# Two-layer transformer on one core: splits after all maxima, first GpSimd addition before the pairs, rows normalised later, a new end of the first layer, and ScalarE copying a fifth block

## What is computed

```python
x = x + ln(attn0(ln(x)))      # 32 query heads of 16, one key/value head, ALiBi bias, causal softmax
x = x + ln(ffn0(ln(x)))       # one 512x512 matrix (block-quantised codes times scales) and a bias
x = x + ln(attn1(ln(x)))      # 32 heads of 128, 8 low-rank key/value heads, partial rotary embedding
x = x + ln(ffn1(ln(x)))       # octonion-structured ternary gate, up and down matrices, silu
```

## Time and profile before

| | |
|---|---|
| median of 3 runs | 2241.18 us (2239.95 to 2243.91) |
| the profiled execution's own time | 2244.26 us |
| span of its profile | 2242.3 us |
| PE busy | 2064.2 us (92%) |
| DVE busy | 1767.8 us (79%) |
| ACT busy | 1389.1 us (62%) |
| POOL busy | 936.3 us (42%) |
| mean granted PE clock | 0.973 of full |

### The profile page before, as it was taken

One profiled execution on the slowest core, in us unless ns is written; L12 is line 12 of the kernel. 1 busy time (PEld: TensorE's weight loads), 2 busy tenths in 40 slices (PEclk: granted clock), 3 DMA queues, 4 the chain that ended last, 5 costly groups with the idle time before them and its releaser, 6 DMA issues. The chain is left out here.

```text
span 2242.3 us, 48569 instructions
## 1 busy us (share of the span) xinstructions
PE 2064.2 (92%) x18563; PEld 1248.5 (56%) x18563; DVE 1767.8 (79%) x3711; ACT 1389.1 (62%) x3037; POOL 936.3 (42%) x901
## 2 busy tenths in 40 slices
PE   7678989898757799999999999999999999988998
PEld 3356666566524466665666666556565665534443
DVE  5689999999665787787787778878778877977665
ACT  2455665656545687787687777777777776762222
POOL 0067786879833233333323323333323323253221
PEclk9799999999878999999999999999999999999999
DMA  5201010101113444434453454354354344520100
GB/s 203 79 16 36 13 51 17 54 10 47 27 65 89 84 68 91 90 68 93 89 94 66 90 100 82 68 91 91 68 94 90 66 85 78 102 76 19 38 20 38
DMA packets 390214, 153.81 MB, mean 69 GB/s; under 512 B 358544, under 2 KB 369424, under 8 KB 387936
## 3 DMA queue, kind: packets, MB, share of 16 engines
q1 hardware_dynamic: 389984, 150.71, 30.9%
HBM read 48.69 MB, written 11.53 MB: 27 GB/s over the span
## 5 line engine op out<-in xcount | busy, mean ns | idle before, releaser
L1777 POOL TENSOR_TENSOR q_in_sbuf<-q_in_sbuf,sinq 128x512 f32<-128x512 f32 x128 | 162.6, 1271 | 722.0 <-ACT q_in_sbuf L1909 598.4
L1921 ACT ACTIVATE xp<-xp,nm 128x128 f32<-128x128 f32 (+3 forms) x512 | 281.4, 551 | 199.1 <-DVE nm L2004 199.1
L1803 PE MATMUL bank<-xT_hi,weights_and_hi 128*128 128x512 f16 x1280 | 382.5, 381 | 7.5 <-DVE yacc L2019 4.8
L823 ACT ACTIVATE weights_and_hi<-bank,unit 128x512 f32<-128x512 f32 x320 | 214.3, 688 | 175.0 <-PE bank L622 172.5
L1886 ACT ACTIVATE probs_hi<-xp,rl 128x128 f16<-128x128 f32 (+3 forms) x512 | 245.2, 550 | 67.9 <-DVE rl L2024 64.3
L1973 DVE SCALAR_TENSOR_TENSOR probs_lo<-xp,rl,probs_hi 128x128 f16<-128x128 f32 (+3 forms) x512 | 282.6, 614 | 0.0
L1981 DVE TENSOR_TENSOR q1T_lo<-qf,q1T_hi 128x512 f16<-128x512 f32 x128 | 88.5, 691 | 225.0 <-ACT q1T_hi L1900 225.0
L2004 DVE CUSTOM_DVE_ANT_0 xp<-bank,mask,cs 128x128 f32<-128x128 f32 (+3 forms) x512 | 250.5, 546 | 0.0
L1803 PE MATMUL bank<-xT_lo,weights_and_hi 128*128 128x512 f16 x640 | 243.6, 381 | 0.0
L540 POOL CAST weights_and_hi<-weights_and_hi 128x1024 f16<-128x1024 f32 (+1 forms) x192 | 188.5, 996 | 121.2 <-ACT weights_and_hi L823 120.6
L1803 PE MATMUL bank<-p1T_hi,v_hi 128*128 128x128 f16 x1280 | 221.9, 219 | 3.3 <-DMA p1T_lo<-probs_lo 3.3
(11 more groups left out here) (307 smaller groups left out, 5499.3 us busy)
## 6 DMA issues: line engine op xcount, KB each, us to landing
weights_and_hi<-in_wq SPq DMA_DIRECT2D x8, 1024.0 KB, 5.9
raw_o<-in_wo SPq DMA_DIRECT2D x8, 1024.0 KB, 5.9
x_front<-in_x SPq DMA_DIRECT2D x4, 1024.0 KB, 6.5
q_stack<-q_hi SPq DMA_DIRECT2D x64, 64.0 KB, 2.6
xb<-in_x SPq DMA_DIRECT2D x4, 1024.0 KB, 5.3
wup<-in_wup SPq DMA_DIRECT2D x3, 1024.0 KB, 12.1
fused_scratch<-weights_and_hi SPq DMA_DIRECT2D x12, 256.0 KB, 3.0
x_scratch<-xb SPq DMA_DIRECT2D x3, 1024.0 KB, 4.3
```

The lines of the kernel that those rows point to most:

```text
L823: act.activation(px[:, p % 2, i, :], bank_of(("x", p, i))[:, :], ACT.Exp, scale=unit[:, 0:1]).then_inc(s_ed, 1)
L1777: pool.tensor_tensor(qs[:, i % 2, :], qs[:, i % 2, :], rope["sink" if u[0] == "k" else "sinq"][:, :], ALU.mult).then_inc(s_rot, 1)
L1803: ins = pe.matmul(out, lhs(a), rhs(c), start=(first and i == 0), stop=(last and i == 2))
L1921: ins = act.activation(x, x, ACT.Exp, scale=-1.0, bias=nm[:, m % 3, t:t + 1], accum_out=ls[:, m % 3, t:t + 1])
```

## The change

1. **Setup.** The four clamps and reciprocals come first, then the constants, then the low halves in a row. PE transposes batch 0's rows before it waits for the next part of `wup`, not after. SP no longer waits for the stored tiles at the end of the setup. The wait is moved to the first exponential and to the later loads, which needs the slopes' scratch in a tensor of its own.
2. **POOL.** One small addition (`first_sum`) at the start of the layer, whose result nothing reads.
3. **Fifth block.** ACT copies its high half one step later, behind the first exponential of the next pair. POOL keeps the subtraction, one step later, ahead of its casts.
4. **Rows.** ACT normalises rows 0, 1 at the start and 2, 3 at the end of step +2 (before: 0, 1 at the end of +1, and 2, 3 at the start of +2).
5. **End.** The steps stop at n = 73. The last transposes of heads (`o`, 3) come a step earlier, batch 2's last `f` tile a step later, and in the steps after the last scores the reciprocals of the sums come before the evacuations. Batch 2's `a2` and `n3` and the last batch's `y` are woven into the tail by hand on all engines. The last batch has its own residual rows `xl` (the memory of the front rows, loaded early), its own `yl` (that of the normed heads) and own statistics. The tail uses all eight banks. The next layer's splits move to its end.

```diff
@@ split_matrices, DVE
                 dve.reciprocal(rg[:, i:i + 1], gm[:, i:i + 1]).then_inc(s_rg, 1)
-                dve.wait_ge(s_rg, i + 1)
+            after.get("vector", nothing)(dve)
+            dve.wait_ge(s_rg, len(jobs))
+            for i, job in enumerate(jobs):
                 dve.wait_ge(s_hi, i + 1)
@@ FusedUpProjections
         for i, (m, n) in enumerate(self.tiles):
-            pe.wait_ge(self.s_ld[n + 1], 16)
             if i == 4:
                 rows.transpose(pe, self.bank[4:8])
+            pe.wait_ge(self.s_ld[n + 1], 16)
...
-        sp.wait_ge(self.s_o, 16 * len(self.tiles))
@@ layer0, POOL
+                pool.tensor_tensor(first_sum[:, :], C["mhalf"][:, 0:TT], C["mhalf"][:, 0:TT], ALU.add)
...
-                    for i, (c0, c1) in enumerate(((0, 2), (2, 4), (4, 5))):
+                    for i, (c0, c1) in enumerate(((0, 2), (2, 4))):
                         pool.wait_ge(*emptied[("x", p, c1 - 1)])
                         pool.tensor_copy(ph[0][:, p % 2, c0:c1, :], px[:, p % 2, c0:c1, :]).then_inc(s_wh, 1)
-                    pool.wait_ge(s_wh, 3 * p + 3)
+
+                def last_weights_lo(p):
+                    pool.wait_ge(s_w4, p + 1)
                     pool.tensor_tensor(ph[1][:, p % 2, 4, :], px[:, p % 2, 4, :], ph[0][:, p % 2, 4, :],
                                        ALU.subtract).then_inc(s_wc, 1)
@@ layer0, ACT
+                    if (p, i) == (0, 0):
+                        act.wait_ge(K0.s_stored, K0.STORED)
...
+                def last_weights_hi(p):
+                    if p >= 2:
+                        act.wait_ge(s_pf, p - 1)
+                    act.wait_ge(*emptied[("x", p, 4)])
+                    act.activation(ph[0][:, p % 2, 4, :], px[:, p % 2, 4, :], ACT.Copy).then_inc(s_w4, 1)
...
+                        if i == 0 and 0 <= n - X_LAG - 1 < NP:
+                            last_weights_hi(n - X_LAG - 1)
...
-                        for u in norms_at(n - 2) if i < 2 else norms_at(n - 1) if i > 2 else ():
-                            normalise(u, i + 2 if i < 2 else i - 3)
+                        for u in norms_at(n - 2) if i != 2 else ():
+                            normalise(u, i if i < 2 else i - 1)
@@ layer0, order of the end
-        STEPS = range(-6, NP + 17)
+        STEPS = range(-6, NP + 10)
...
+            late = {("f", LAST - 1, TT - 1): 41, ("o", LAST, TT - 1): 24}
...
-        END = ([("g1", LAST, 0), ("g2", LAST, 0)] + [(k, LAST, t) for k, t in (("n2", 0), ("n2", 1), ("f", 0), ("n2", 2), ("f", 1), ("n2", 3), ("f", 2),
-                                          ("f", 3))] + [("n3", LAST, t) for t in range(TT)])
+        L = LAST
+        END = [("y", L, 0), ("y", L, 1), ("g1", L, 0), ("y", L, 2), ("y", L, 3), ("g2", L, 0), ("n2", L, 0), ("n2", L, 1),
+               ("f", L, 0), ("f", L, 1), ("n2", L, 2), ("n2", L, 3), ("n3", L - 1, 0), ("f", L, 2), ("n3", L - 1, 1),
+               ("n3", L, 0), ("n3", L - 1, 2), ("f", L, 3), ("n3", L, 1), ("n3", L - 1, 3), ("n3", L, 2), ("n3", L, 3)]
...
-        groups = {"s": banks[0:3], "x": banks[3:5], "rest": banks[5:8], "end": banks[0:5]}
+        groups = {"s": banks[0:3], "x": banks[3:5], "rest": banks[5:8], "end": banks}
...
+        sc.sems.append(K0.s_stored)
```

More of the change, by code:

```diff
@@ L352, in others @@
             for kind in ("y", "f"):
-                for t, w in enumerate(BACK[kind]):
-                    b = at(n, w)
-                    if b is not None and has(kind, b):
-                        out.append((kind, b, t))
+                out += [(kind, b, t) for t in range(TT) for b in range(B)
+                        if n == PAIRS * b + offset(kind, b, t) and has(kind, b)]
             if at(n, FRONT["V"]) is not None:
@@ L363, in others @@
                         out += [(kind, b, 2 * i), (kind, b, 2 * i + 1)]
-            for t, w in enumerate(BACK["o"]):
-                if at(n, w) is not None:
-                    out.append(("o", at(n, w), t))
+            out += [("o", b, t) for t in range(TT) for b in range(B) if n == PAIRS * b + offset("o", b, t)]
             return out
@@ L490, in _ @@
                     b = at(n, NORM["a2"] + 4)
[L491 to L493 removed]
+                    if b is not None and has("a2", b):
+                        store_rows(b)
                     if n == NP + V_LAG:
@@ L712, in fill @@
                     else:
-                        rows = {"n1": xf, "n2": ya, "n3": yb}[kind]
-                        if u in END:
+                        rows = yl if (kind, b) == ("n3", LAST) else {"n1": xf, "n2": ya, "n3": yb}[kind]
+                        if b == LAST and kind != "n1":
                             ready = (s_tn, tail_no[1 if kind == "n2" else 3, u[2]])
@@ new lines, in _ @@
+                ahead = LAST - 1
+                evacuate(("y", LAST, 0))
+                for t in range(3):
+                    normalise(("a2", ahead), t)
+                evacuate(("y", LAST, 1))
+                tail_rows(0, 0)
+                evacuate(("y", LAST, 2))
+                tail_rows(0, 1)
+                evacuate(("y", LAST, 3))
+                normalise(("a2", ahead), 3)
+                tail_rows(1, 0)
+                tail_rows(0, 2)
+                hi4(("n2", LAST, 0))
@@ new lines, in _ @@
+                hi4(("n3", ahead, 1))
+                hi4(("n3", LAST, 0))
+                N1.high(act, 0)
+                tail_rows(3, 1)
+                hi4(("n3", ahead, 2))
+                normalise(("n3", ahead), 3)
+                tail_rows(2, 2)
+                hi4(("n3", LAST, 1))
+                tail_rows(2, 3)
+                hi4(("n3", ahead, 3))
+                tail_rows(3, 2)
+                N1.high(act, 1)
+                hi4(("n3", LAST, 2))
+                tail_rows(3, 3)
@@ L884, in _ @@
+                hi4(("n3", LAST, 3))
             @block.vector
@@ L1080, in _ @@
[L1080 to L1100 removed]
+                    tail_statistics(k + 1, t, xl)
@@ new lines, in _ @@
+                N1.reciprocals(dve, bank_of(("g2", LAST, 0)))
+                tail_y(3)
+                ahead_statistics(3)
+                lo4(("n2", LAST, 0))
+                variance(("n3", ahead))
+                tail_add(0, 2)
+                lo4(("n2", LAST, 1))
+                tail_add(0, 3)
+                tail_f(0)
+                tail_f(1)
+                lo4(("n2", LAST, 2))
+                tail_add(2, 0)
+                lo4(("n2", LAST, 3))
+                lo4(("n3", ahead, 0))
@@ L1102, in layer0 @@
+                tail_add(2, 1)
+                tail_f(2)
+                lo4(("n3", ahead, 1))
+                lo4(("n3", LAST, 0))
+                tail_f(3)
+                lo4(("n3", ahead, 2))
+                lo4(("n3", LAST, 1))
+                tail_add(2, 2)
+                lo4(("n3", ahead, 3))
+                tail_add(2, 3)
+                N1.low(dve, 0)
+                lo4(("n3", LAST, 2))
+                N1.low(dve, 1)
+                lo4(("n3", LAST, 3))
         clear(nc, sc.sems)
@@ L2557, in build @@
                                {"sync": other_loads, "tensor": lambda pe: fuse.multiply(pe, rows),
-                                "scalar": lambda act: fuse.copy(act, range(4, len(fuse.tiles)))},
-                               {"vector": rows_and_constants})
+                                "scalar": lambda act: fuse.copy(act, range(4, len(fuse.tiles))),
+                                "vector": rows.constants},
+                               {"vector": rows_low})
                 clear(nc, ss.sems)
```

199 lines of the change are left out of this document (124 added, 75 removed).

## The result

The changed kernel takes 2226.1 us (median of 4 runs, 2223.77 to 2229.5), the kernel before beside it 2240.56 (2237.97 to 2243.91). The ratio is 0.9937, 95% interval 0.9921 to 0.9953. So the change gains 14.5 us, where 30.7 were forecast: the side was right, the size less than half, outside the range of 2197 to 2224. The profiled execution took 2229.5 us (span 2227.7). One of the seven executions of before_sum, a kernel further down, took 4235.99 us; without it its median would be 2235.1 us, not the 2235.63 given there.

The account below looks back on a forecast made before the run. The prediction took DVE to set the pace in the steady pairs (95% busy), PE close behind (90%), and the end to be a chain of waits. Its terms summed to -30.7 us, from 2241.2 to 2210 us, range 2197 to 2224.

Parts of the forecast that it names:

- Term 1: Setup: reordered work lets the layer begin at 57.6 us instead of 66.4, with PE last; -8.8 us.
- Term 2: Start of the layer: POOL's added instruction takes its 7.13 us stall early, so DVE's 5.88 us wait goes; -5.9 us.
- The rival in which it does nothing: Start of the layer: the stall comes back at the old place, the addition gains 0; 2216 us, chance 0.02.
- Term 3: Steady pairs, 125 to 560 us: old DVE waits on POOL go, new meetings of their subtractions cost more; +2 us.
- the stated ends of -12 and +14: Steady pairs: -12 if copies lose nothing, +14 if meetings cost more and PE falls behind.
- The old lock waits: Steady pairs: 17.9 us in 29 DVE instructions that begin during POOL's fifth-block subtraction, expected to go.
- The meetings that the prediction priced at 20 us: Steady pairs: POOL's subtraction against DVE's second subtraction, 6 us, and around DVE's copies of maxima, 14 us.
- The copy on ACT: Steady pairs: 64 new copies of 0.6 us each lie in ACT's idle time; 0, or +4 in the bad case.
- Term 4: Pairs after the last scores: seven fifth-block casts of 7.3 us leave POOL's chain, part of the wait stays; -4.5 us.
- Term 5: End of the layer: weaving the last two batches fills DVE's waits; -14 us, with +0.5 for a second barrier.
- PE behind ACT: Rival, steady pairs: ACT's new copy holds up exponentials and so PE's banks, +19 on the forecast; 2229 us, chance 0.02.
- Slower than before: Rival, pairs: POOL's subtraction comes first against one of DVE's in every pair, 74 us; +23, 2264 us, chance 0.03.

Follow-up runs that it names:

- before_sum: The kernel before with only POOL's small addition (`first_sum`) behind the memsets: 2235.63 us, ratio 0.9967.
- before_setup: The kernel before with only the setup's part of the change: 2233.26 us, ratio 0.9962.
- lo_ahead: The changed kernel with POOL's fifth-block subtraction moved ahead of the two casts of its step: 2204.4 us, ratio 0.9838.
- the part alone: The kernel before with only the fifth block's part: copy on ACT, POOL's subtraction behind the next pair's casts: 2260.88 us, ratio 1.008.
- lo_first: The changed kernel with POOL's fifth-block subtraction first in its step, also ahead of row additions, roots and head scaling: 2200.46 us, ratio 0.9819.
- copy_early: lo_first with ACT's fifth-block copy ahead of the next pair's first exponential instead of behind it: 2210.51 us, ratio 0.9856.
- rows_back: The changed kernel with the rows normalised as before, the fifth block's part left in: 2225.24 us, ratio 0.993.
- pool_late: lo_ahead with POOL making the fifth block's high half itself right ahead of the subtraction, ACT copying nothing: 2218.09 us, ratio 0.9892.

## Why the prediction was wrong

- **Term 1, setup (-8.8): right.** The layer begins at 57.42 (forecast 57.6), the first reciprocal stands at 33.30, and PE is last. Here the last low half of DVE and the transposes with the 64 matmuls:

```profile
47.27 2.33 DVE L200 SCALAR_TENSOR_TENSOR wf_lo<-raw_wf,rg,wf_hi 128x2048 f16<-128x2048 f32 x1
```

```profile
24.85 1.91 PE L1323 MATMUL fu_bank<-ident,x_front 128*128 128x128 f32 x16
27.67 27.73 PE L1413 MATMUL fu_bank<-wup,wdk 128*128 128x512 f32 x64 [0.91 <-DMA wup<-in_wup]
```

  The low halves end at 49.6, the matmuls at 55.4, as worked out from the earlier trace rows (50.3 and 55.2). The second barrier costs 0.7 us (DVE's wait behind it is 1.78 where it was 1.09), forecast 0.5.
- **Term 2, the addition (-5.9): right.** 6.5 by the markers. The rival in which it does nothing is out: POOL has no wait of this kind behind 100 us. Both terms together came out 2.5 us larger than forecast at pair 0 (17.2 against 14.7), 1.4 of them in before_setup alone (10.2 against 8.8) and 0.6 in before_sum. The clock granted from 66 to 125 us rose from 0.79 to 0.91 in the changed kernel, but in before_setup it was 0.80, so it does not account for the 1.4 there. That part stays open.
- **Term 3, steady pairs (+2): the step that failed.** The working placed POOL's subtraction ahead of the casts and priced it only against DVE. It said "POOL's work in a pair falls by a cast, the subtraction moves to its front". In fact, as the rows of 505.53 to 511.99 show, the subtraction moved behind two casts of the next pair, and the consumer on its heels was PE, which runs ahead of DVE. I never asked when PE needs the result: before, it was ready a step earlier. +19.2 was measured, with 19.9 us of PE's waits for this subtraction. Where the prediction thought it to stand (lo_ahead), the stage came to -1.9, within the stated ends of -12 and +14 and 4 us from the +2. The old lock waits went in part: DVE's mean fell from 1384 ns to 1313, and its copy's from 644 to 357:

```profile
L1102 DVE TENSOR_TENSOR weights_lo<-weights_and_hi 128x1024 f16<-128x1024 f32 x111 | 145.7, 1313 | 0.3 <-issue 0.3
L1110 DVE COPY mx<-mp 128x8 f32<-128x8 f32 x13 | 4.6, 357 | 0.5
```

  The time did not go with them, because PE was late. In lo_ahead the excess of both over 1.17 and 0.18 us, from pair 0 to 54, is 28.1 us where it was 29.4 before: -1.3, close to the +2, but in part by luck. The meetings that the prediction priced at 20 us (POOL's subtraction against DVE's second one and the copies) hold less: from 110 to 560 us 6.9 us in 28 of DVE's subtractions, most of them 0.17 each, near the 0.15 of the forecast, and some 2 us in the copies. POOL's casts, which it had left out, hold 13.3 us in 23 (3.9 in 33 before). One of these, a row of POOL and one of DVE in lo_ahead:

```profile
194.21 1.03 POOL L563 CAST weights_and_hi<-weights_and_hi 128x1024 f16<-128x1024 f32 x1
```

```profile
194.36 1.95 DVE L1102 TENSOR_TENSOR weights_lo<-weights_and_hi 128x1024 f16<-128x1024 f32 x1
```

  DVE's ends at 196.31, 1.07 us behind the cast's end. The copy on ACT was priced at 0, with the casts' lateness as its cover. Behind the first exponential nothing in the runs speaks against that; ahead of it the copy costs 10 us.
- **Term 4, pairs after the last scores (-4.5): right in kind, lost to the same cause.** +0.4 in the changed kernel, -5.0 as soon as the subtraction stands ahead of the casts, -7.9 when it is first.
- **Term 5, the end (-14 + 0.5): right in sum, -12.8.** One of its steps failed: PE's first `y` product was to come 2.4 us earlier, but it stands 5.1 us behind the last pair's reciprocal (617.70 to 622.81) where it stood 4.1 behind (615.33 to 619.42), since PE works on two `f` products first (from 617.20 to 622.81). The chain from there to the second layer made up for it, 13.8 us shorter. DVE's wait of 10.0 us for `ya` is gone, and its waits from 617 us to the barrier's wait of 1.8 are

```profile
DVE yb L1074 <- PE bank L642: 3.0, 2, 2.1
DVE cs L2195 <- PEq L103: 1.8, 1, 1.8
DVE xT_lo L1031 <- ACT xT_hi L826: 1.5, 2, 1.0
DVE heads_normed L1181 <- PE bank L642: 0.9, 2, 0.7
```

- **The rivals.** "PE behind ACT" gave 2229, the nearest in size, with 0.02. Its consequence was right (PE stands still, the clock falls) and its cause wrong: PE waits for POOL. "Slower than before" had the right instruction, but took the loss to be DVE's blocked time, and the meetings became fewer. With +20 us in the pairs against 30 gained elsewhere the kernel as a whole stays faster, and the part alone is slower.

With term 3 at +19.2 and term 4 at +0.4 in place of +2 and -4.5, the forecast's own sum is -30.7 + 17.2 + 4.9 = -8.6, and with the 2.5 us more at pair 0 -11.1, against -10.4 in the profile's first layer and -14.5 by the medians. The 4 us between these two are a spread between executions. The profiled one of the changed kernel is the slowest of its four, 3.4 us above the median, though its second layer is as short as any (1554.2), so its first layer was longer than in a median one. That +19.2 is some us too high for a usual execution fits with it: the other two kernels with the late subtraction have +13.6 and +15.8. No run shows in which stage the 3.4 us lie.

## What to carry to other kernels

When a step is moved on an engine, read its new neighbours in the instruction order itself, not in the words of the change. Then ask of every consumer, not only of the pacing engine, when it wants the result: an engine that runs ahead of the pace, like PE here, turns lateness that DVE would never notice into a chain around all four. And where two engines exclude each other, ask which of the two has to wait, not only how often they meet: from lo_ahead to lo_first DVE's mean falls from 1429 to 1348 ns, POOL's rises from 1497 to 1559, and the kernel is 3.9 us faster. It is not all that counts: the changed kernel has the lowest mean of DVE of them (1313) and is the slowest.

## What the runs showed that I had not expected

- One idle gap of PE of 2.8 us was followed by 10 us at a granted clock of 0.83. Over 125 to 560 us the changed kernel, with its 22 waits of 19.9 us in total, has 0.95 against 0.99; lo_ahead has 0.98. A higher clock alone is not the gain: copy_early has 1.00 there and is 10 us slower than lo_first, which has 0.98.
- Pairs 0 to 54 repeated between the profiles of before, before_sum and before_setup, which have the same pair code, to 0.2 and 0.4 us, while the second layer varies by up to 4 us. But changed kernel and rows_back differ by 5.6 us there and by 0.9 in their medians. So a stage length from one profile needs the medians beside it.
- POOL's casts to f16 hold DVE's two-input subtraction as POOL's subtraction does (1.95 us at 194.36 in lo_ahead). And a cast of 0.6 us can cost more by where it puts the instruction behind it than by itself: in pool_late DVE's mean rose from 1429 to 1559 ns.
- Not tried: the parts of the new end one by one, and what the waits of PE would have cost at an unchanged clock. The same matmuls took 16.8 us more from pair 0 to 54, but at the full clock PE might have waited for some of that.
